# Attention with sixteen-wide heads: the sums over the keys of two key tiles issued one behind the other, with room for four tiles of exponentials

## The chip, the cores and the metric

The kernel runs on one NeuronCore of one Trainium2 chip. The metric is the time of the device for the whole program, in microseconds (us). The kernel before takes 2302.59 us, the median of three runs (2300.83 to 2303.88). All of the program's work is one launch: twelve layers of a decoder, one behind the other.

## The reference, cut to what matters

Twelve sublayers, each `x = x + f(layernorm(x))`, with B = 2 sequences, T = 512 queries and C = 256 channels. Three of them are attentions that this change reaches, all with 16 heads of 16 channels:

```python
# first self attention: causal, with linear position biases (ALiBi)
# third self attention: a band, |i - j| <= 32
band = jnp.abs(idx[:, None] - idx[None, :]) <= WINDOW // 2
scores = jnp.where(band[None, None], scores, -jnp.inf)
attn = jax.nn.softmax(scores, axis=-1)
out = jnp.einsum('bhqk,bhkd->bhqd', attn, v)
...
# last cross attention: 512 queries against 1024 keys, no mask
scores = jnp.einsum('brqd,brkd->brqk', qh, kh) * scale
weights = jax.nn.softmax(scores, axis=-1)
out = jnp.einsum('brqk,brkd->brqd', weights, vh)
```

## The kernel before, in words

The program is a chain of stages with a barrier between them. Within a stage each engine has its own instruction list, written out by hand, and waits on semaphores. Four of the stages are made by `quad_attention_stage` (L3085): `a0a` (first self attention, causal), `a2a` (third self attention, banded), `a2x` (third cross attention, with a full mask, which brings its own buffer `probs`) and `a3x` (last cross attention). The change does nothing in `a2x`.

A stage works through U = 8 units; a unit is one group of four heads of one sequence. A unit has KT key tiles of 128 keys: 4 in `a0a` and `a2a`, 8 in `a3x`. Key tiles are counted through the whole stage as n, up to N = 32, 32 and 64. In a unit three things happen:

- **Rows.** For every query tile and head one matmul gives scores with queries on partitions (`row`, L3233, in the self attentions followed by a mask matmul, L3236), and VectorE takes the maximum of each (`row_maximum`, L3392). These only serve to find the shift of the softmax. They run more than one unit ahead: `lead` rows (44 in `a3x`) are done before the loop. Their results lie in `ring`, three banks of PSUM, so that a row matmul waits until the maximum three places back has been taken (`wait_for_bank`). When a unit's rows are done, VectorE makes `most` (L3398), TensorE turns it (`turn_most`, L3243) and ScalarE negates it (`negate`, L3349) and a DMA puts it into the queries' stack. `turn_most` and a turn of the finished sums (`turn_u`, L3287, read by VectorE at L3413 and L3416) take a place of the ring too.
- **Scores.** For key tile n, in two halves of two heads each, `score(n, half)` (L3260, in the self attentions with the mask at L3265) puts keys on partitions into `scores_T`, which has one place for each half. So the scores of n + 1 wait until ScalarE has taken the exponentials of the same half of n (`exp`, L3336).
- **Sums.** `value(n)` (L3279) multiplies the exponentials with the values, four matmuls (float32, one for each head) that write 32 partitions of `u` each, side by side. After a unit's last tile ScalarE copies `u` out (`u_out`, L3356) before the next unit's first sum may begin.

Everything around the change is set by the order of TensorE's list. For each n and half it is: the scores of n + 1, two rows, `turn_u` or `turn_most` if this is their slot (slot s is 2 times the key tile in the unit plus the half; `turn_u_at` is 4; `turn_most_at` is 10 in `a3x` and 1 in the self attentions), and in the first half the sums of n - 1. The exponentials have R = 3 places in `pT`, so `exp(n, 0)` waits for the sums of n - 3. In `a3x` two float32 weight matrices are also quantised by VectorE behind its last maximum (L3440 to L3456), for which TensorE does one small matmul (L3317) in the third tile from the end.

Of the kernel before, what the change touches and what calls it, by code (L numbers as in the profile page):

```python
# [243 lines left out]

def project_stage(core, name, turned_jobs, value_jobs, values="h d", loads=(), first=(), room=None, R=5,
                  padding=None, rounding=None, early=(), spread=False):
# [21 lines left out]
    with stage(core, name) as st:  # L268
# [9 lines left out]
        if room is None:  # L278
            x32 = st.sb("x32", [P, R, 512])
            left = st.sb("left", [P, R, 512])  # L280
            hml = st.sb("hml", [P, R, 3, 512], BF16)
            vout = st.sb("vout", [P, RV, V]) if value_jobs else None
        else:
            x32, left = (room[:, x * R * 512:(x + 1) * R * 512].rearrange("p (r t) -> p r t", r=R) for x in range(2))
            hml = room[:, R * 1024:R * 1792].bitcast(BF16).rearrange("p (r c t) -> p r c t", r=R, c=3)
            vout = room[:, R * 1792:R * 1792 + RV * V].rearrange("p (r c) -> p r c", r=RV)
# [2798 lines left out]
def quad_attention_stage(core, name, nkey, bufs, q_parts, k_parts, v_scr, ao, keys_of, queries_of, lead, turn_u_at,  # L3085
# [13 lines left out]

    assert len(loads) <= GROUPS * B
    nc = core.nc
    KT = nkey // P
# [3 lines left out]
    N = U * KT  # L3108
    HALVES = 2 * KT
    rows = []  # L3110
    for qt in range(QT):
        k0, n = keys_of(qt)
# [3 lines left out]
    NR = len(rows)  # L3116
    assert NR == 2 * HALVES
    assert nkey // 512 == 1 + max(r[4] for r in rows)
    R = 3
    NSTACK = 16 * (2 * len(RUNS) + (2 if extra else 0))  # L3120
    PER = NR + 2

# [13 lines left out]
    with stage(core, name) as st:  # L3136
# [34 lines left out]
        def first_rows(u, s):  # L3171

            r = lead + NR * u + 2 * s
            return range(r, min(r + 2, U * NR))

        with nc.Block() as block:
# [39 lines left out]
            def _(pe):  # L3216
# [7 lines left out]
                def row(r):  # L3224
                    u, i = divmod(r, NR)
                    qt, h, k0, n, part = rows[i]
                    out = ring[:, row_place(r) % 3, 0:n]
                    if i == 0:
                        stack_ready(pe, u)
                    wait_for_bank(row_place(r))  # L3230
                    lhsT = qs[0:K - 1, u % nbuf, h, qt * P:(qt + 1) * P]
                    rhs = ks[0:K - 1, u % nbuf, h, k0:k0 + n]
                    mm = nc.tensor.matmul(out, lhsT, rhs, start=True, stop=True, skip_group_check=True)  # L3233
                    if key_mask is not None or full is not None:
                        m0, mask = (k0, full[0][:, qt, k0:k0 + n]) if key_mask is None else key_mask(qt)
                        mm = nc.tensor.matmul(out[:, m0 - k0:m0 - k0 + mask.shape[1]], core.ident_bf[:, :], mask,  # L3236
                                              start=False, stop=True, skip_group_check=True)
                    mm.then_inc(rowed, 1)

                def turn_most(u):  # L3240
                    pe.wait_ge(most, u + 1)
                    wait_for_bank(most_place(u))
                    nc.tensor.transpose(ring[0:HG4 * QT, most_place(u) % 3, 0:P], mcol[:, u % 2, :], core.ident[:, :]  # L3243
                                        ).then_inc(most_turned, 1)

                def score(n, half):
                    u, kt = divmod(n, KT)
                    q0, w = queries_of(kt)
                    if kt == 0 and half == 0:
                        stack_ready(pe, u)  # L3250
                        pe.wait_ge(shift_in[u % nbuf], 16 * (u // nbuf + 1))
                    if n and full is not None:
                        pe.wait_ge(masked, 2 * (n - 1) + half + 1)
                        pe.wait_ge(copied, 2 * (n - 1) + half + 1)
                    elif n:
                        pe.wait_ge(expd, 2 * (n - 1) + half + 1)
                    for j in range(2):
                        h = 2 * half + j
                        out = sT[:, half, j, :]
                        mm = nc.tensor.matmul(out[:, 0:w], ks[0:K, u % nbuf, h, kt * P:(kt + 1) * P],  # L3260
                                              qs[0:K, u % nbuf, h, q0:q0 + w], start=True, stop=True,
                                              skip_group_check=True)
                        if query_mask is not None:
                            for m0, mask in query_mask(kt):
                                mm = nc.tensor.matmul(out[:, m0 - q0:m0 - q0 + mask.shape[1]], core.ident_bf[:, :],  # L3265
                                                      mask, start=False, stop=True, skip_group_check=True)
                    mm.then_inc(scored, 1)

                def value(n):
                    u, kt = divmod(n, KT)  # L3270
                    q0, w = queries_of(kt)
                    if kt == 0:
                        pe.wait_ge(v_in[u % 2], 16 * (u // 2 + 1))
                        if u:
                            pe.wait_ge(u_moved, u)
                    pe.wait_ge(expd, 2 * (n + 1))
                    for h in range(HG4):
                        hs = slice(32 * h, 32 * h + 32)
                        mm = nc.tensor.matmul(up[hs, q0:q0 + w], vs[:, u % 2, kt, hs], pT[:, n % R, h, 0:w],  # L3279
                                              start=(kt == 0), stop=True, skip_group_check=True)  # L3280
                    mm.then_inc(valued, 1)
# [17 lines left out]
                for n in range(N):  # L3299
                    u, kt = divmod(n, KT)  # L3300
                    for half in range(2):
                        s = 2 * kt + half
                        if n + 1 < N:
                            score(n + 1, half)
                        for r in first_rows(u, s):
                            row(r)
                        if s == turn_u_at and u:
                            turn_u(u - 1)
                        if s == turn_most_at and u + 1 < U:
                            turn_most(u + 1)  # L3310
                        if half == 0 and n >= 1:
                            value(n - 1)
                        if quant is not None and n == N - 3 and half == 1:
                            pe.wait_ge(weight_step, 2)
                            pe.wait_ge(row_most, U * NR)
                            pe.wait_ge(shift_ready, U)
                            nc.tensor.matmul(sums, core.ones[:, :], part[:, :], start=True, stop=True  # L3317
                                             ).then_inc(weighed, 1)
                value(N - 1)
                turn_u(U - 1)  # L3320

# [594 lines left out]
```

## Time and profile before

| what | us |
|---|---|
| median of three runs | 2302.59 (2300.83 to 2303.88) |
| the profiled execution | 2292.74 |
| its span in the profile | 2290.9 |
| TensorE busy | 1857.9 (81%) |
| VectorE busy | 1476.2 (64%) |
| ScalarE busy | 1072.9 (47%) |
| GpSimd busy | 830.4 (36%) |
| stage `a0a`, from about 45 to 157 | 112 |
| stage `a2a`, from about 1256 to 1344 | 88 |
| stage `a3x`, from about 1949 to 2183 | 234 |

The page gives busy time of each engine over the whole span, which averages over stages with different limits. What bounds the three stages is read from the timeline of each engine: start of each instruction, its length, and in brackets how long its engine sat idle before it and what released it. Matmuls overlap in the pipeline, so the distance of two starts says more than a length.

### The profile page before, as it was taken

Reading aid. Unit: us, or ns where it says so; the run is one execution under the profiler, and the core shown is the slowest. Engines: PE = TensorE matmul, PEld = TensorE weight load, DVE = VectorE, ACT = ScalarE, POOL = GpSimd, SP = SyncE. Lnnn points to the kernel's source line nnn. Section 1 sums busy time; section 2 is a strip of 40 time slices with the busy share of each in tenths; the row PEclk is TensorE's granted clock in tenths of the full one; section 3 lists DMA queues with packets and bytes.
Section 4 is the critical chain, followed back from the end, with each engine's and each line's share of the span. In section 5 each row is a group of like instructions: output and inputs, shape, how many; then the busy total and the mean of one; then the engine's idle time right before and its main releaser. Section 6 shows DMA issues by size and latency. Waiting matters only on the chain. (4 is left out here: it accounts for less than half of the span.)

```text
span 2290.9 us, 32146 instructions
## 1 busy us (share of the span) xinstructions
PE 1857.9 (81%) x11356; PEld 937.0 (41%) x11379; DVE 1476.2 (64%) x2551; ACT 1072.9 (47%) x1818; POOL 830.4 (36%) x751
## 2 busy tenths in 40 slices
PE   5888979999785677677896787999789776999954
PEld 3444423333453444445583552333257433222223
DVE  4643266663766999985435548999454464777676
ACT  2453124444333444542344343888833433366646
POOL 1000035554245999993204012666640412000012
PEclk9999989999986989987898888999889887699977
DMA  6602551210039014003425813332044401443000
GB/s 193 162 26 87 192 174 47 65 46 1 19 103 201 15 30 78 2 1 113 156 73 186 185 54 89 80 70 49 19 176 156 142 10 34 98 95 68 10 1 19
DMA packets 172353, 190.50 MB, mean 83 GB/s; under 512 B 14820, under 2 KB 138799, under 8 KB 171287
## 3 DMA queue, kind: packets, MB, share of 16 engines
q1 hardware_dynamic: 169124, 180.07, 28.5%
q0 software_dynamic: 3072, 8.39, 1.2%
q8 instruction: 93, 1.52, 0.3%
q14 instruction: 64, 0.52, 0.1%
HBM read 124.04 MB, written 68.30 MB: 84 GB/s over the span
## 5 line engine op out<-in xcount | busy, mean ns | idle before, releaser
L3381 POOL TENSOR_TENSOR a2x_masked<-a2x_masked,tall_rows 128x512 f32<-128x512 f32 x128 | 163.3, 1276 | 111.4 <-ACT a2x_masked L3343 111.4
L1398 ACT ACTIVATE experts<-a1x_scores 128x1024 f32<-128x1024 f32 x128 | 124.1, 1021 | 164.5 <-PE a1x_scores L1329 164.5
L3392 DVE TENSOR_REDUCE a3x_row_most<-a3x_ring 128x1 f32<-128x512 f32 x256 | 159.3, 682 | 43.5 <-PE a3x_ring L3233 43.5
L3392 DVE TENSOR_REDUCE a2x_row_most<-a2x_ring 128x1 f32<-128x512 f32 x256 | 162.4, 679 | 7.0 <-DMA pad_scr<-wide_rows 5.3
L1435 POOL TENSOR_TENSOR a1x_tree<-experts 128x1024 f32<-128x1024 f32 x64 | 150.4, 2350 | 32.2 <-ACT experts L1398 32.2
L671 POOL TENSOR_TENSOR a0x_pair_sums<-a0x_probs_T 128x1024 f32<-128x1024 f32 x48 | 114.7, 2390 | 130.1 <-ACT a0x_probs_T L800 102.7
L854 DVE TENSOR_REDUCE ctx_then_heads<-a0x_rows 128x2 f32<-128x1024 f32 x88 | 107.7, 1224 | 82.6 <-PE a0x_rows L689 82.4
L1367 DVE TENSOR_TENSOR experts<-experts,a1x_inverse_total 128x2048 f32<-128x2048 f32 x64 | 145.7, 2276 | 4.2 <-ACT a1x_inverse_total L1411 4.2
L3336 ACT ACTIVATE a3x_probs_T<-a3x_scores_T 128x1024 f32<-128x1024 f32 x128 | 123.2, 1018 | 48.4 <-PE a3x_scores_T L3260 48.4
L1318 PE MATMUL a1x_scores<-a1x_qs,a1x_ks 96*128 96x128 bf16 x1024 | 92.4, 243 | 58.7 <-ACT experts L1398 45.1
L3336 ACT ACTIVATE wide_rows<-a2x_masked 128x1024 f32<-128x1024 f32 x128 | 135.8, 1061 | 1.4 <-POOL a2x_masked L3381 1.4
L800 ACT ACTIVATE a0x_probs_T<-a0x_scores_T 128x1024 f32<-128x1024 f32 x96 | 98.4, 1025 | 77.5 <-PE a0x_scores_T L715 60.5
L1377 DVE TENSOR_REDUCE a1x_most<-a1x_scores 128x128 bf16<-128x2048 f32 x43 | 98.5, 2292 | 33.2 <-PE a1x_scores L1318 33.2
L1329 PE MATMUL a1x_scores<-a1x_most,a1x_minus_ident 128*128 128x512 bf16 x256 | 72.7, 410 | 56.6 <-DVE a1x_most L1383 30.0
L1318 PEld LDWEIGHTS a1x_scores<-a1x_qs,a1x_ks 96*128 96x128 bf16 x1024 | 68.3, 109 | 107.7 <-ACT experts L1398 78.5
L3233 PE MATMUL a2x_ring<-a2x_ks,a2x_qs 97*128 97x512 bf16 x256 | 99.3, 388 | 13.2 <-DMA a2x_qs<-in_ones_bf 10.2
L711 PE MATMUL a0x_scores_T<-ctx_then_heads 64*128 64x512 f32 x384 | 102.3, 611 | 0.7 <-ACT ctx_then_heads L806 0.7
L3404 DVE TENSOR_TENSOR a2x_masked<-a2x_scores_T,tall_rows 128x512 f32<-128x512 f32 x128 | 87.6, 685 | 23.3 <-ACT wide_rows L3336 14.8
L3233 PE MATMUL a3x_ring<-a3x_ks,a3x_qs 96*128 96x512 bf16 x256 | 94.1, 427 | 8.0 <-DMA a3x_qs<-q_scr 8.0
L728 PE MATMUL a0x_u<-a0x_probs_T,a0x_vs 128*64 128x512 f32 x384 | 92.8, 605 | 0.0
L3343 ACT COPY a2x_masked<-a2x_scores_T 128x512 f32<-128x512 f32 x128 | 74.8, 585 | 37.3 <-PE a2x_scores_T L3260 31.1
L1344 PE MATMUL a1x_u<-experts,a1x_vs 128*32 128x128 f32 x2048 | 85.4, 318 | 6.1 <-DVE experts L1367 6.1
(676 smaller groups left out, 4268.3 us busy)
## 6 DMA issues: line engine op xcount, KB each, us to landing
v_scr<-p0x_vout SPq DMA_DIRECT2D x24, 256.0 KB, 2.0
k_scr<-p0x_x SPq DMA_DIRECT2D x24, 256.0 KB, 2.3
ctx_then_heads<-k_scr SPq DMA_DIRECT2D x8, 768.0 KB
a0x_vs<-v_scr SPq DMA_DIRECT2D x8, 768.0 KB, 5.1
experts<-in_L_ffn_w SPq DMA_DIRECT2D x8, 768.0 KB, 6.6
v_scr<-experts SPq DMA_DIRECT2D x16, 256.0 KB, 2.2
a1x_vs<-v_scr SPq DMA_DIRECT2D x16, 256.0 KB, 5.2
v_scr<-m1f_vout SPq DMA_DIRECT2D x16, 256.0 KB, 2.8
```

What stands on the lines that cost most here:

```text
L671: nc.gpsimd.tensor_tensor(pair[:, n // 2 % RP, :, :], pT[:, (n - 1) % R, :, :], pT[:, n % R, :, :], ALU.add).then_inc(paired, 1)
L711: nc.tensor.matmul(sT[:, n % 2, h, :], ks[hs, u % 3, kt * P:(kt + 1) * P], qs[hs, u % 3, :], start=True, stop=False, skip_group_check=True)
L854: nc.vector.tensor_reduce(rm[:, qt, :, c], row_psum(r)[:, :, :], AX.X, ALU.max).then_inc(row_most, 1)
L1318: mm = nc.tensor.matmul(sp_[:, g % 3, i, j, :], ks[0:96, h, kt * P:(kt + 1) * P], qs[0:96, h, qt * P:(qt + 1) * P], start=(j == 0), stop=F ...
L1367: nc.vector.tensor_tensor(ex[:, n % E, :, :], ex[:, n % E, :, :], rp[:, 0, :].unsqueeze(1).to_broadcast([P, H, P]), ALU.mult).then_inc(nor ...
L1377: nc.vector.tensor_reduce(mx[:, n % 2, :], src, AX.X, ALU.max).then_inc(most, 1)
L1398: nc.scalar.activation(ex[:, n % E, 8 * half:8 * half + 8, :], sp_[:, g % 3, :, :, :].rearrange("p i j q -> p (i j) q"), ACT.Exp).then_inc ...
L1435: nc.gpsimd.tensor_tensor(tree[:, :, :], e[:, 0:8], e[:, 8:16], ALU.add).then_inc(folded, 1)
L3233: mm = nc.tensor.matmul(out, lhsT, rhs, start=True, stop=True, skip_group_check=True)
L3336: nc.scalar.activation(pT[:, n % R, 2 * half:2 * half + 2, 0:w], src, ACT.Exp).then_inc(expd, 1)
L3381: nc.gpsimd.tensor_tensor(sm[:, i % 2, 1, :], sm[:, i % 2, 1, :], full[1][:, i // 2 % KT, :], ALU.add).then_inc(pool_masked, 1)
L3392: nc.vector.tensor_reduce(rm[:, u % 2, h * QT + qt:h * QT + qt + 1, part], ring[:, row_place(r) % 3, 0:n], AX.X, ALU.max).then_inc(row_mos ...
```

## The change

Where the stage has its own buffer of exponentials (`a0a`, `a2a`, `a3x`), the buffer has four places in place of three, and TensorE issues the sums of two key tiles together: in the first half of every even n the sums of n - 2 and n - 1, and none at odd n. At the end the sums of the last two tiles follow. Lines move by one to six.

```diff
-    R = 3
+    R = 4 if probs is None else 3
...
-                        if half == 0 and n >= 1:
+                        if half == 0 and probs is not None and n >= 1:
+                            value(n - 1)
+                        if half == 0 and probs is None and n >= 2 and n % 2 == 0:
+                            value(n - 2)
                             value(n - 1)
...
+                if probs is None:
+                    value(N - 2)
                 value(N - 1)
                 turn_u(U - 1)
```

TensorE's list in `a3x` about the turn of the maxima, before (L3260 scores, L3233 rows, L3279 sums, L3243 `turn_most`):

```order
L3279 MATMUL a3x_u<-a3x_probs_T,a3x_vs 32x512 x4
L3260 MATMUL a3x_scores_T<-a3x_qs,a3x_ks 128x512 x2
L3233 MATMUL a3x_ring<-a3x_ks,a3x_qs 128x512 x2
L3260 MATMUL a3x_scores_T<-a3x_qs,a3x_ks 128x512 x2
L3233 MATMUL a3x_ring<-a3x_ks,a3x_qs 128x512 x2
L3243 MATMUL a3x_ring<-ident,a3x_most 16x128
L3279 MATMUL a3x_u<-a3x_probs_T,a3x_vs 32x512 x4
L3260 MATMUL a3x_scores_T<-a3x_qs,a3x_ks 128x512 x2
```

The same place in the changed kernel, on to the next sums (L3261, L3234, L3280, L3244 are the same lines, moved by one):

```order
L3280 MATMUL a3x_u<-a3x_probs_T,a3x_vs 32x512 x8
L3261 MATMUL a3x_scores_T<-a3x_qs,a3x_ks 128x512 x2
L3234 MATMUL a3x_ring<-a3x_ks,a3x_qs 128x512 x2
L3261 MATMUL a3x_scores_T<-a3x_qs,a3x_ks 128x512 x2
L3234 MATMUL a3x_ring<-a3x_ks,a3x_qs 128x512 x2
L3244 MATMUL a3x_ring<-ident,a3x_most 16x128
L3261 MATMUL a3x_scores_T<-a3x_qs,a3x_ks 128x512 x2
L3234 MATMUL a3x_ring<-a3x_ks,a3x_qs 128x512 x2
L3261 MATMUL a3x_scores_T<-a3x_qs,a3x_ks 128x512 x2
L3234 MATMUL a3x_ring<-a3x_ks,a3x_qs 128x512 x2
L3280 MATMUL a3x_u<-a3x_probs_T,a3x_vs 32x512 x8
```

Before, four rows lay between one tile's sums and the next, and one tile's sums stood directly behind `turn_most`. Now eight rows lie between two pairs of sums, and behind `turn_most` come scores.

The end of `a3x`, where no rows are left, TensorE before:

```order
L3279 MATMUL a3x_u<-a3x_probs_T,a3x_vs 32x512 x4
L3260 MATMUL a3x_scores_T<-a3x_qs,a3x_ks 128x512 x4
L3279 MATMUL a3x_u<-a3x_probs_T,a3x_vs 32x512 x4
L3260 MATMUL a3x_scores_T<-a3x_qs,a3x_ks 128x512 x4
L3279 MATMUL a3x_u<-a3x_probs_T,a3x_vs 32x512 x4
```

and in the changed kernel:

```order
L3280 MATMUL a3x_u<-a3x_probs_T,a3x_vs 32x512 x8
L3261 MATMUL a3x_scores_T<-a3x_qs,a3x_ks 128x512 x8
L3280 MATMUL a3x_u<-a3x_probs_T,a3x_vs 32x512 x8
L3261 MATMUL a3x_scores_T<-a3x_qs,a3x_ks 128x512 x8
```

Two halves of scores between the sums have become four. The lists of the other engines keep their order.

## Rows read from the trace of the kernel before

**Rows 1.** The page, busy time of each engine over the span.
```profile
PE 1857.9 (81%) x11356; PEld 937.0 (41%) x11379; DVE 1476.2 (64%) x2551; ACT 1072.9 (47%) x1818; POOL 830.4 (36%) x751
```

**Rows 2.** Windows of `a0a`, `a2a`, `a3x`: length, busy of PE, PEld, DVE, ACT, POOL, clock, DMA.
```profile
45.00:157.00 112.00, 92.83 (x808) 47.28 (x808) 61.05 (x152) 50.20 (x82) 0.00 (x0) 0.92 0.49 121
1256.00:1344.00 88.00, 73.15 (x808) 49.13 (x808) 44.20 (x150) 35.52 (x82) 0.00 (x0) 0.87 0.64 158
1949.00:2183.00 234.00, 215.07 (x1068) 58.98 (x1069) 176.84 (x290) 129.51 (x147) 0.00 (x0) 0.92 0.29 65
```

**Rows 3.** Timeline of PE in `a3x`, one regular key tile: start, length, instructions.
```profile
2069.11 1.06 PE L3279 MATMUL a3x_u<-a3x_probs_T,a3x_vs 128*32 128x512 f32 x8
2070.11 0.60 PE L3260 MATMUL a3x_scores_T<-a3x_qs,a3x_ks 97*128 97x512 bf16 x2
2070.55 0.60 PE L3233 MATMUL a3x_ring<-a3x_ks,a3x_qs 96*128 96x512 bf16 x2
2070.98 0.59 PE L3260 MATMUL a3x_scores_T<-a3x_qs,a3x_ks 97*128 97x512 bf16 x2
...
2072.03 1.07 PE L3279 MATMUL a3x_u<-a3x_probs_T,a3x_vs 128*32 128x512 f32 x8
```

**Rows 4.** The same timeline in cuts: second pass of the sums; the fourth row.
```profile
2069.56 0.61 PE L3279 MATMUL a3x_u<-a3x_probs_T,a3x_vs 128*32 128x512 f32 x4
...
2071.72 0.39 PE L3233 MATMUL a3x_ring<-a3x_ks,a3x_qs 96*128 96x512 bf16 x1
```

**Rows 5.** Timeline of DVE in the same stretch.
```profile
2070.97 2.48 DVE L3392 TENSOR_REDUCE a3x_row_most<-a3x_ring 128x1 f32<-128x512 f32 x4 [0.44 <-PE a3x_ring L3233]
2073.89 0.69 DVE L3392 TENSOR_REDUCE a3x_row_most<-a3x_ring 128x1 f32<-128x512 f32 x1 [0.45 <-PE a3x_ring L3233]
```

**Rows 6.** Timelines of PE and ACT in `a3x` about the turn of the maxima.
```profile
2075.46 0.28 PE L3243 MATMUL a3x_ring<-ident,a3x_most 128*16 128x128 f32 x1 [0.43 <-DVE a3x_most L3398]
2075.67 1.06 PE L3279 MATMUL a3x_u<-a3x_probs_T,a3x_vs 128*32 128x512 f32 x8
2077.00 0.61 PE L3260 MATMUL a3x_scores_T<-a3x_qs,a3x_ks 97*128 97x512 bf16 x2 [0.27 <-ACT a3x_probs_T L3336]
...
2078.93 1.06 PE L3279 MATMUL a3x_u<-a3x_probs_T,a3x_vs 128*32 128x512 f32 x8
...
2075.95 1.00 ACT L3336 ACTIVATE a3x_probs_T<-a3x_scores_T 128x1024 f32<-128x1024 f32 x1
```

**Rows 7.** Timeline of PE in `a3x` where one unit's sums end.
```profile
2058.66 1.07 PE L3279 MATMUL a3x_u<-a3x_probs_T,a3x_vs 128*32 128x512 f32 x8
...
2061.36 0.61 PE L3260 MATMUL a3x_scores_T<-a3x_qs,a3x_ks 97*128 97x512 bf16 x2 [0.66 <-ACT a3x_probs_T L3336]
```

**Rows 8.** Timelines of PE and ACT in the last unit of `a3x`, without rows.
```profile
2157.78 1.04 PE L3260 MATMUL a3x_scores_T<-a3x_qs,a3x_ks 97*128 97x512 bf16 x4
...
2161.95 0.39 PE L3260 MATMUL a3x_scores_T<-a3x_qs,a3x_ks 97*128 97x512 bf16 x1
...
2158.43 2.99 ACT L3336 ACTIVATE a3x_probs_T<-a3x_scores_T 128x1024 f32<-128x1024 f32 x3 [0.42 <-PE a3x_scores_T L3260]
```

**Rows 9.** Timelines of PE and DVE at the end of `a3x`.
```profile
2174.17 0.28 PE L3317 MATMUL a3x_ring<-a3x_weight_part,ones 128*128 128x2 f32 x2
...
2179.43 0.65 PE L3287 MATMUL a3x_ring<-ident,a3x_u_sb 128*128 128x128 f32 x4 [0.71 <-ACT a3x_u_sb L3356]
...
2181.83 0.25 DVE L3413 RECIPROCAL a3x_inverse<-a3x_ring 128x16 f32<-128x16 f32 x1
```

**Rows 10.** Timeline of PE in `a0a`, start of a unit.
```profile
115.74 0.28 PE L3243 MATMUL a0a_ring<-ident,a0a_most 128*16 128x128 f32 x1 [0.36 <-DVE a0a_most L3398]
117.06 0.28 PE L3260 MATMUL a0a_scores_T<-a0a_qs,a0a_ks 103*128 103x256 bf16 x1 [1.05 <-ACT a0a_probs_T L3336]
```

**Rows 11.** Timeline of PE in `a2a`, the one long wait.
```profile
1317.10 0.29 PE L3260 MATMUL a2a_scores_T<-a2a_qs,a2a_ks 97*128 97x160 bf16 x1 [2.95 <-issue]
```

## The prediction

> **What bounds the kernel now.** I read the page first: TensorE is busy 81% of the span, VectorE 64% [rows 1]. That is an average; the change touches three stages, so the windows of those come next [rows 2]. In each TensorE is the busiest engine: 92.8 of 112 us in `a0a`, 73.2 of 88 in `a2a`, 215.1 of 234 in `a3x`. But in `a3x` VectorE has 176.8 us of its own, and the two are coupled through a ring of three banks. So the timeline of a regular key tile in `a3x` decides. Its period is 2.93 us, from the sums at 2069.11 to those at 2072.03 [rows 3], and it can be walked through as one loop over two engines:
>
> - sums start to the next scores: 1.00 (2069.11 to 2070.11) [rows 3];
> - scores to the first maximum on VectorE: 0.86 (2070.11 to 2070.97) [rows 3, 5];
> - that maximum to the fourth row, which waits for its bank: 0.75 (2070.97 to 2071.72) [rows 4, 5];
> - fourth row to the sums: 0.32 (2071.72 to 2072.03) [rows 3, 4].
>
> Together 2.93. VectorE's four maxima take (2.48 - 0.68) / 3 = 0.60 from start to start, 0.68 being one alone [rows 5], so it works 2.48 of the 2.93 and idles 0.44 while the sums run. The slack of VectorE is thin, and the reader should see that it lies exactly in the time of the sums.
>
> **What the change gives: one change of array shape less per pair.** Matmuls of 512 columns start 0.22 apart (two scores from 2070.11, two rows from 2070.55, two scores from 2070.98) [rows 3]. From the fourth row to the sums it is 0.32, so 0.10 is lost on entering. The sums are two passes, the second 0.45 after the first (2069.11, 2069.56) [rows 3, 4]. The next scores come 0.55 after the start of the second pass, so about 0.10 is lost on leaving. A second tile's sums directly behind the first should start like a further pass: 0.45 + 0.45 = 0.91, where alone it would cost 0.91 + 0.10 + 0.10. So a pair saves 0.20, if nothing else is in the way. No row shows one tile's sums behind another's at full pace; the bounds are 0.91 (pass behind pass) and 1.10 (as when alone). I take 0.91, since the two passes already load different weights.
>
> The fourth place for exponentials costs no instruction. It removes a possible wait of ScalarE for the sums three tiles back, which now come up to a tile later; I put it at nothing either way. VectorE, GpSimd and the queues keep their lists; the DMAs of SP wait for scores or sums of a whole unit and move along with these.
>
> **`a3x`, regular pairs: slower by 0.38.** Eight rows now lie between two pairs of sums. The ring holds three, so the eighth row must wait for the fifth maximum. Walking the same loop: sums to scores 0.91 + 1.00, scores to first maximum 0.86, to the end of the fifth 0.75 + 4 x 0.60 = 3.14, to the sums 0.32. That is 6.23, against 2 x 2.93 = 5.85. TensorE alone would be there sooner: sixteen matmuls of 0.22 and the entering give 3.6 from the scores where the loop gives 0.86 + 3.14 + 0.32 = 4.32. What happened is plain: during two tiles of sums VectorE has at most three banks of work, 1.8 us, and it gets nothing new for 1.91 + 0.86. Its idle time per two tiles rises from 0.88 to 1.35, and TensorE waits for it later.
>
> **`a3x`, the pair with `turn_most`: slower by 0.91.** There the chain first maximum, `most`, turn, negate, exponential, scores takes 3.11 (2073.89 to 2077.00) [rows 5, 6]. Before, a tile's sums (2075.67) lay inside it, while ScalarE worked at 2075.95, and TensorE still idled 0.27. Now scores stand there, waiting for the same exponential, and the sums are paid elsewhere at 0.91. The rest is the same length in both: 1.00 + 0.86 ahead, 1.92 from 2077.00 to the sums at 2078.93.
>
> **`a3x`, the pair at the end of a unit: about +0.06.** Sums to the scores behind `u_out` take 2.70 (2058.66 to 2061.36) [rows 7]. Now: 0.91 + 2.70 + 0.86 + 0.75 + 2 x 0.60 for the eighth row, 0.60 for the bank of `turn_u`, 0.56 for it and the entering: 7.58. Before: from 2058.66 to 2.93 ahead of 2069.11, which is 7.52.
>
> A unit of eight tiles has two regular pairs and one of each other: 0.76 + 0.91 + 0.06 = 1.73. Rows last for 53 of the 64 tiles, 6.5 units: **+11.2 us**.
>
> **`a3x`, the last five pairs, without rows: 0.89 each.** Before, two tiles take 4.17 (2157.78 to 2161.95) [rows 8]; ScalarE needs 4 x 0.92 = 3.7 of it, and one tile's sums always run beside its exponentials. Now: a pair of sums 1.91, the scores behind it and their landing 0.65, an exponential 0.92, a second to its end 1.05, the last scores and entering 0.53: 5.06. **+4.4 us.** Against this the end of the stage: VectorE's quantising starts with the small matmul at 2174.17 and holds up the last reciprocal until 2181.83, 7.66 later, though TensorE's turn was done at 2179.43 + 0.65 = 2180.08 [rows 9]. Now the small matmul stands one place further from the end, 6.9 ahead of the turn's end (by 1.0, since one tile's sums moved behind it), so 1.0 of those 1.75 is hidden: **-1.0**. `a3x` in all: +14.6.
>
> **`a0a` and `a2a`: faster.** Maxima are shorter here (128 to 512 columns in `a0a`, at most 192 in `a2a`) and each row has two matmuls, so VectorE is busy only half of the window [rows 2] and the ring does not bind on a pair. Seven units keep rows: 14 pairs x 0.20 = -2.7 in each (0.19 before rounding). In `a0a` TensorE also waits 0.36 for VectorE ahead of `turn_most` in each unit, with 1.05 for ScalarE behind it [rows 10]; the sums that stood ahead of this place now follow the 512-column rows, VectorE gets these earlier, and I take this 0.36 as gone in seven units: -2.5. The last units have no rows, and by the same count as in `a3x` three and a half pairs each cost more: 0.5 each in `a0a` (widths of 320 on average, where 512 cost 0.89), 0.3 in `a2a`: +1.8 and +1.1. So **`a0a` -3.4, `a2a` -1.5**. In `a2a` TensorE waits 2.95 once for a DMA [rows 11]; if that landing does not come earlier with the rest, half of the gain is lost: 0.8.
>
> **The sum.** +14.6 - 3.4 - 1.5 = +9.7. Against the profiled execution's 2292.74 that is 2302.4; the median of the runs stands 9.85 above that execution, and I expect the same of the changed kernel: **2312.3 us**, slower by 0.42%.
>
> The Trainium skill warns of this side: TensorEngine Tiling (Array Packing), Performance Considerations, PSUM Bottleneck, says that tiling speeds up TensorE and not the emptying of PSUM, which may then bound. By it the pairs in `a3x` gain nothing or lose, and those in the self attentions keep their gain; the trace agrees, with 0.60 a maximum in `a3x` and VectorE half idle in `a0a` and `a2a` [rows 2, 5]. The page has a rule for the other side too, which stands with the first rival.
>
> **Rivals.**
>
> *Faster, the ring does not bind.* If VectorE kept its pace through the pair, all 64 pairs would save 0.20, and nothing would be lost at the turns: -12.6, so 2290. For it: TensorE is the busiest engine everywhere, 0.20 per pair is in the trace. Against it: the eighth row's wait. It decides at a maximum of (5.85 - 3.09 - 0.15) / 5 = 0.52 per start, 3.09 being 1.91 + 0.86 + 0.32 and 0.15 a maximum's tail and wait; above it a pair loses, and 0.60 is measured. The Trainium skill has the rule for this rival: TensorEngine Tiling (Array Packing), Key Properties, says that a change of tiling mode drains TensorE. The 0.10 on entering and on leaving agree. Chance 0.04.
>
> *Slower still, the second sums cost as much as alone.* Then 1.10 in place of 0.91, 64 times: +12.3 more, 2325. Half of it, 2318, is as likely. For it: no row of such a sequence. Against it: pass behind pass at 0.45. Chance 0.10 together.
>
> *Hardly slower.* Part of the loss in `a3x` is not there: if TensorE's wait for the turn's chain is filled, or VectorE's lateness in `a0a` gives back more, `a3x` falls to about +8 and the sum to +3: 2306. Chance 0.08, and 0.03 of it below 2304.
>
> *The change does not do what it says.* The order of both programs excludes it: eight sums in one row where four stood.
>
> **How the numbers follow.** Forecast 2308 to 2317 with 0.78; the rivals 0.04, 0.10 and 0.08. The range that leaves two in ten out is 2306 to 2320: it takes in half of the rival on the second sums, and the bounds of `a0a` and `a2a` (nothing gained there gives 2317). A measurement of this kernel tells about 0.2%, 4.6 us, from no change: faster than 2298.0 has 0.04, between 2298.0 and 2307.2 has 0.08, slower 0.88.
>
> **What would show each step.** In `a3x`: sums of 16 records whose third pass starts 0.45 after the second; a regular pair of 6.2; the eighth row released by VectorE; idle of TensorE of about 1 us behind `turn_most`, ended by ScalarE; two tiles in 5.06 at the end; a window of some 248 us. In `a0a` some 108.5 and no wait ahead of `turn_most`. The prediction is wrong if a regular pair in `a3x` is below 5.85, or if the sums of a pair take 2.1.

## The result

The changed kernel takes 2314.53 us (median of seven runs, against 2303.88 for seven runs of the kernel before beside it); the ratio is 1.0057 with a 95% interval of 1.0032 to 1.0083, so +13.1 us, between +7.4 and +19.1. The prediction said +9.7 and 2312.3. One of the seven executions took 9211 us and is left out of the ratio. The profiled execution is a long one, 2328.88, so its length is no measure and only single stretches are read from it. A second profiled execution of the same kernel (the first experiment) took 2313.5 in its span.

The page of the changed kernel, engines over the span, answers to [rows 1]:

```profile
PE 1872.6 (80%) x11356; PEld 948.5 (41%) x11379; DVE 1474.7 (63%) x2551; ACT 1071.6 (46%) x1818; POOL 831.0 (36%) x751
```

The same instructions, and the same work on VectorE and ScalarE. Windows about `a0a`, `a2a` and `a3x` in it answer to [rows 2]; columns as there:

```profile
44.00:156.00 112.00, 90.43 (x808) 48.32 (x808) 61.74 (x152) 49.93 (x82) 0.00 (x0) 0.92 0.52 121
1260.00:1348.00 88.00, 70.20 (x812) 50.88 (x812) 44.58 (x152) 36.38 (x83) 0.40 (x2) 0.88 0.62 161
1955.00:2220.00 265.00, 232.57 (x1070) 65.34 (x1070) 175.56 (x290) 129.43 (x147) 0.10 (x1) 0.85 0.24 57
```

All of the loss is in `a3x`. From its first matmul to its last it was 230.1 us before; here it is 262.0, and 248.7 in the second execution.

**A regular pair.** Timeline of PE in `a3x` of the changed kernel, from one pair of sums to the next; beside [rows 3]:

```profile
2054.04 1.92 PE L3280 MATMUL a3x_u<-a3x_probs_T,a3x_vs 128*32 128x512 f32 x16
2055.90 0.61 PE L3261 MATMUL a3x_scores_T<-a3x_qs,a3x_ks 97*128 97x512 bf16 x2
2056.34 0.60 PE L3234 MATMUL a3x_ring<-a3x_ks,a3x_qs 96*128 96x512 bf16 x2
2056.78 0.59 PE L3261 MATMUL a3x_scores_T<-a3x_qs,a3x_ks 97*128 97x512 bf16 x2
2057.21 0.69 PE L3234 MATMUL a3x_ring<-a3x_ks,a3x_qs 96*128 96x512 bf16 x2
2057.74 0.60 PE L3261 MATMUL a3x_scores_T<-a3x_qs,a3x_ks 97*128 97x512 bf16 x2
2058.17 0.38 PE L3234 MATMUL a3x_ring<-a3x_ks,a3x_qs 96*128 96x512 bf16 x1
2058.70 0.39 PE L3234 MATMUL a3x_ring<-a3x_ks,a3x_qs 96*128 96x512 bf16 x1 [0.15 <-DVE a3x_row_most L3398]
2058.93 0.60 PE L3261 MATMUL a3x_scores_T<-a3x_qs,a3x_ks 97*128 97x512 bf16 x2
2059.36 0.38 PE L3234 MATMUL a3x_ring<-a3x_ks,a3x_qs 96*128 96x512 bf16 x1
2059.90 0.39 PE L3234 MATMUL a3x_ring<-a3x_ks,a3x_qs 96*128 96x512 bf16 x1 [0.15 <-DVE a3x_row_most L3398]
2060.22 0.64 PE L3280 MATMUL a3x_u<-a3x_probs_T,a3x_vs 128*32 128x512 f32 x4
```

The period is 6.18, against 5.85 for two single tiles. The sixth and the eighth row stand alone in their rows because they wait for VectorE. The same timeline cut at the third and at the fourth pass of the sums, and VectorE (DVE) in the stretch:

```profile
2054.93 0.61 PE L3280 MATMUL a3x_u<-a3x_probs_T,a3x_vs 128*32 128x512 f32 x4
...
2055.35 0.61 PE L3280 MATMUL a3x_u<-a3x_probs_T,a3x_vs 128*32 128x512 f32 x4
...
2056.76 4.28 DVE L3398 TENSOR_REDUCE a3x_row_most<-a3x_ring 128x1 f32<-128x512 f32 x7 [1.60 <-PE a3x_ring L3234]
```

The third pass starts 0.89 and the fourth 1.31 after the first, at 2054.04. So the passes behind the first step of 0.45 follow at 0.43, also from one tile to the other, and the second tile's sums cost 0.86 and not 0.91 (1.86 from the pair's start to the scores at 2055.90, where one tile's took 1.00). VectorE starts at 2056.76, 0.86 behind the scores, and then works without a break; from its start to the eighth row it is 3.14, as the prediction has it.

**The turn of the maxima.** PE and ACT, beside [rows 6]:

```profile
2064.50 0.28 PE L3244 MATMUL a3x_ring<-ident,a3x_most 128*16 128x128 f32 x1 [0.43 <-DVE a3x_most L3404]
2066.04 1.03 PE L3261 MATMUL a3x_scores_T<-a3x_qs,a3x_ks 97*128 97x512 bf16 x2 [1.26 <-ACT a3x_probs_T L3342]
...
2064.99 1.90 ACT L3342 ACTIVATE a3x_probs_T<-a3x_scores_T 128x1024 f32<-128x1024 f32 x2
```

TensorE idles 1.26 where it did a tile's sums before. And something else is there: two scores take 1.03 and not 0.61. The windows on either side show why; the clock is the number behind POOL:

```profile
2059.00:2065.90 6.90, 5.20 (x30) 1.42 (x28) 5.30 (x10) 2.51 (x5) 0.00 (x0) 1.00 0.02 4
2065.90:2072.70 6.80, 6.66 (x24) 1.63 (x24) 2.58 (x4) 3.04 (x4) 0.00 (x0) 0.50 0.00 1
```

The granted clock is 0.50, 1.2 GHz, for 6.8 us, from the end of the idle on. Such falls came in five units in a row of this execution, and a sixth came where the rows end:

```profile
2185.40:2192.20 6.80, 6.05 (x22) 1.14 (x23) 0.00 (x0) 3.53 (x4) 0.00 (x0) 0.50 0.00 1
```

Four of the five units take 30.8 or 30.9, where one without a fall takes 27.7 and one of the kernel before 26.1 (distances of a unit's first exponential to the next unit's).

### The profile page after: what moved, and what is told of

Same layout as the page of the kernel before. It is cut to its first block and busy times, and to the rows that moved or that the text cites. A ratio compares the mean times of both kernels' runs of the same rounds, so it can differ in the third digit from the quotient of the medians.

```text
span 2327.0 us, 32143 instructions
## 1 busy us (share of the span) xinstructions
PE 1872.6 (80%) x11356; PEld 948.5 (41%) x11379; DVE 1474.7 (63%) x2551; ACT 1071.6 (46%) x1818; POOL 831.0 (36%) x751
## 5 line engine op out<-in xcount | busy, mean ns | idle before, releaser
L1318 PEld LDWEIGHTS a1x_scores<-a1x_qs,a1x_ks 96*128 96x128 bf16 x1024 | 70.3, 111 | 107.2 <-ACT experts L1398 77.9
L3234 PE MATMUL a3x_ring<-a3x_ks,a3x_qs 96*128 96x512 bf16 x256 | 102.6, 448 | 12.9 <-DMA a3x_qs<-q_scr 8.0
L3234 PE MATMUL a2x_ring<-a2x_ks,a2x_qs 97*128 97x512 bf16 x256 | 99.1, 387 | 13.3 <-DMA a2x_qs<-in_ones_bf 10.3
L3261 PE MATMUL a3x_scores_T<-a3x_qs,a3x_ks 97*128 97x512 bf16 x256 | 84.3, 417 | 17.7 <-ACT a3x_probs_T L3342 17.7
```

Of the source, the lines that this page charges most:

```text
L1318: mm = nc.tensor.matmul(sp_[:, g % 3, i, j, :], ks[0:96, h, kt * P:(kt + 1) * P], qs[0:96, h, qt * P:(qt + 1) * P], start=(j == 0), stop=F ...
```

## Experiments

Stage lengths below run from the first matmul of a stage to its last. The theory has three parts, all in `a3x`: the ring of three banks starves VectorE during a pair; the sums leave the shadow of the turn's chain; and in the last unit ScalarE starves. Against these it sets 0.20 saved per pair. The rivals are named in each expectation.

**The changed kernel once more.** No edit.

> The changed kernel once more. Its first profiled execution has three events at which the granted clock of TensorE falls to half for 6.8 us that repeat in every unit of a3x, and a window of 262 us for the stage where the step by step count gave 248.6. If these falls always come with the idle behind turn_most, this execution has a3x at 260 us or more again and the program at about 2328. If they come in some executions only, this one has a3x near 248 and the program near 2313, with regular pairs of 6.2 us and 1.5 us of idle behind turn_most as before.

Measured: ratio 1.0065 (1.0038 to 1.0093), median 2313.4. `a3x` 248.7, regular pairs 6.17, idle behind `turn_most` 1.26. The long falls of the clock come in some executions only; in this one there are three falls, of 3.4 us each. Two of them in windows:

```profile
2062.60:2066.00 3.40, 3.40 (x19) 0.70 (x17) 1.84 (x4) 1.15 (x2) 0.00 (x0) 0.50 0.00 0
2175.20:2178.60 3.40, 3.40 (x17) 0.57 (x10) 0.00 (x0) 0.95 (x2) 0.00 (x0) 0.51 0.00 0
```

The idles of 1.26 ended at 2061.09 and 2173.49, 1.5 and 1.7 ahead of these. The other four turns have the same idle of 1.26 and no fall behind it. A unit with a short fall took 29.3, so such a fall costs 1.6. This execution also has the last unit clean; PE from one pair of sums to the next there, beside [rows 8]:

```profile
2187.97 1.92 PE L3280 MATMUL a3x_u<-a3x_probs_T,a3x_vs 128*32 128x512 f32 x16
2189.83 1.04 PE L3261 MATMUL a3x_scores_T<-a3x_qs,a3x_ks 97*128 97x512 bf16 x4
2191.55 0.60 PE L3261 MATMUL a3x_scores_T<-a3x_qs,a3x_ks 97*128 97x512 bf16 x2 [0.68 <-ACT a3x_probs_T L3342]
2192.46 0.61 PE L3261 MATMUL a3x_scores_T<-a3x_qs,a3x_ks 97*128 97x512 bf16 x2 [0.31 <-ACT a3x_probs_T L3342]
2193.00 1.92 PE L3280 MATMUL a3x_u<-a3x_probs_T,a3x_vs 128*32 128x512 f32 x16
```

5.03 for two tiles, 4.17 before: the exponentials follow the scores one by one while no sums are left to fill TensorE.

**Pairs in the self attentions alone.**

```diff
-    R = 4 if probs is None else 3
+    paired = probs is None and KT == 4
+    R = 4 if paired else 3
...
-                        if half == 0 and probs is not None and n >= 1:
+                        if half == 0 and not paired and n >= 1:
...
-                        if half == 0 and probs is None and n >= 2 and n % 2 == 0:
+                        if half == 0 and paired and n >= 2 and n % 2 == 0:
...
-                if probs is None:
+                if paired:
                     value(N - 2)
```

> Pairs and four places in a0a and a2a alone; a3x as in the kernel before. Theory (array shape changes saved, VectorE not in the way in these two stages): a0a shorter by 3.4 and a2a by 1.5, so 4.9 us below the kernel before. Rival (the self attentions wait for ScalarE and the DMA queue and give nothing back): within 1 us of the kernel before, and the whole of the change's loss is then smaller in a3x than counted.

Measured: ratio 0.9985 (0.9969 to 1.0002), -3.4 us, between -7.1 and +0.5. That holds both the theory's -4.9 and nothing. The profile is clearer. A regular unit of `a0a` takes 11.3 where it took 12.1, the wait of 0.36 ahead of `turn_most` [rows 10] is gone in the turns of the third to seventh unit, and a unit of `a2a` takes 8.4 for 8.8. But one wait in `a0a`, of scores that need what DMAs bring (queries, keys and shift of the unit), is longer than in the profile before:

```profile
88.05 0.59 PE L3262 MATMUL a0a_scores_T<-a0a_qs,a0a_ks 103*128 103x512 bf16 x1 [4.03 <-issue]
```

The next run, which has no pairs in `a0a`, has it too:

```profile
87.77 0.59 PE L3262 MATMUL a0a_scores_T<-a0a_qs,a0a_ks 103*128 103x512 bf16 x1 [4.16 <-issue]
```

So it does not need the pairs. It stands in all thirteen profiled executions, 0.44 to 6.06 long (1.25 in the kernel before), and it always ends 40.7 to 43.1 us behind the stage's first matmul. Ahead of it the sixteen DMA engines are busy all the time; a window of the kernel before, with their share (1.11) and GB/s last:

```profile
73.00:85.00 12.00, 10.36 (x100) 5.34 (x97) 7.56 (x20) 6.13 (x10) 0.00 (x0) 1.00 1.11 275
```

So what TensorE saves ahead of this wait, in the first units, it waits away again, and mostly the units behind it can shorten the stage. `a2a` has such a wait too, of 1.65 to 5.13, which ends 58.3 to 61.4 behind its first matmul in all thirteen. With a wait of some 4 in both, `a0a` takes 111.7 here and 114.6 in the next run: 2.9 less, for 3.4 forecast. `a2a` takes 88.4 here, 87.9 and 86.6 in the kernel before and the next run, which have no pairs there, and 85.5 and 86.7 in the two of the changed kernel: its DMA waits vary by more than the pairs give.

**Pairs in `a3x` alone.** As above with `KT == 8`.

> Pairs and four places in a3x alone. Theory (ring of three banks, turn's chain, last unit): a3x longer by 14.6 without falls of the clock, so about 2318, and by up to 32 with them. Rival (the pairs are neutral in a3x, and what was lost is lost in the self attentions): within 2 us of the kernel before.

Measured: ratio 1.0078 (1.0051 to 1.0104), +17.9, between +11.7 and +23.9; `a3x` 248.7, as in the kernel with all pairs. The loss is all here. The number is larger than the change's +13.1, but the intervals overlap widely, and with the -3.4 of the run before it makes +14.5.

**The turn behind a pair of sums.**

```diff
-                                 queries_of=lambda kt: (0, T), lead=44, turn_u_at=4, turn_most_at=10, **stack,
+                                 queries_of=lambda kt: (0, T), lead=44, turn_u_at=4, turn_most_at=12, **stack,
```

> The changed kernel with turn_most of a3x in slot 12 in place of 10, so that a pair of sums stands directly behind it again. Theory (the chain of turn, negate and exponential costs 0.91 per unit only because no sums lie in its shadow): 7 us below the changed kernel, about 2307, TensorE's idle behind turn_most gone, and with it any fall of the clock at this place. Rival (ring alone): the idle only moves to another place, within 2 us of the changed kernel.

Measured: ratio 1.0007 (0.9992 to 1.0023), 2302.63: 10.8 below the changed kernel's 2313.4, and `a3x` 238.5, 10.2 less. PE about the turn:

```profile
2054.90 0.27 PE L3244 MATMUL a3x_ring<-ident,a3x_most 128*16 128x128 f32 x1 [0.30 <-DVE a3x_row_most L3398]
2055.10 1.92 PE L3280 MATMUL a3x_u<-a3x_probs_T,a3x_vs 128*32 128x512 f32 x16
2056.95 0.61 PE L3261 MATMUL a3x_scores_T<-a3x_qs,a3x_ks 97*128 97x512 bf16 x2
```

The scores behind the pair no longer wait. The pair that holds the turn takes 6.96, for 7.75 in the changed kernel and 6.89 before. Two of the three falls of the clock are gone with the idle; one is left in the last unit. A unit takes 26.9 for 27.7: 0.8, where the theory has 0.91. The remainder of the 10.2 is the falls and the end of the stage. The regular pairs stay at 6.17: the rival (ring alone) was right about these and wrong about the rest, since the idle did not come back elsewhere. That the falls went with the idle rests on one profiled execution of this kernel.

**Three places for exponentials.**

```diff
-    R = 4 if probs is None else 3
+    R = 3
```

> The changed kernel with three places for exponentials in place of four. Theory: the fourth place hides nothing; ScalarE's exponentials of a tile would wait for the first of the two sums, but at that time ScalarE has the second half of the tile before to do, so a3x, a0a and a2a keep their lengths within 1 us each (a3x 248.7 from first to last matmul, as in the second look at the changed kernel). Rival: ScalarE is held in each pair, the scores behind the pair come late, and a3x grows by 0.3 per pair or more, 10 us.

One execution: 2319.97, `a3x` 248.7 and every unit of it as in the changed kernel to 0.1, `a0a` 111.6, `a2a` 86.5. The fourth place hides nothing here. The total is from one execution and says no more.

**Maxima at half their size, sums single and in pairs.** Both runs have `turn_most_at=12` in `a3x`, and there take each maximum over 256 of the 512 columns, which leaves that part of the maxima out. The first is the kernel before with these edits, the second the changed kernel.

```diff
                     nc.vector.tensor_reduce(rm[:, u % 2, h * QT + qt:h * QT + qt + 1, part],
-                                            ring[:, row_place(r) % 3, 0:n], AX.X, ALU.max).then_inc(row_most, 1)
+                                            ring[:, row_place(r) % 3, 0:(n // 2 if quant is not None else n)], AX.X, ALU.max).then_inc(row_most, 1)
```

> Sums one tile at a time, as before, but turn_most of a3x in slot 12, and VectorE takes each maximum in a3x over 256 of the 512 columns (the shift of the softmax is then the maximum over half of the keys; this leaves work out). A maximum then takes 0.33 from start to start in place of 0.60. TensorE is the bound of a regular key tile: two tiles in 5.66, and a3x about 26 less rows' time at the start, some 207 to 212 us. It is the partner of the next run.

> The changed kernel's order with turn_most of a3x in slot 12 and maxima in a3x over 256 of 512 columns (leaves the same work out). Theory (0.20 saved per pair where the ring does not bind, by the count it stops binding below 0.52 per maximum): regular pairs of 5.48 against 5.66 in the run before, a3x shorter than there by about 5, the last unit still longer by 3.5. Rival (the loss of a pair has nothing to do with VectorE's pace): regular pairs here are again 0.3 to 0.4 longer than two single tiles.

Measured: 2274.31 single (ratio 0.9878, 0.9852 to 0.9905), 2264.74 in pairs (0.9843, 0.9819 to 0.9867). `a3x` 206.3 and 201.2. PE and DVE of the first in a regular tile:

```profile
2042.95 1.06 PE L3279 MATMUL a3x_u<-a3x_probs_T,a3x_vs 128*32 128x512 f32 x8
...
2045.79 0.64 PE L3279 MATMUL a3x_u<-a3x_probs_T,a3x_vs 128*32 128x512 f32 x4
...
2044.81 0.76 DVE L3392 TENSOR_REDUCE a3x_row_most<-a3x_ring 128x1 f32<-128x256 f32 x2 [1.21 <-PE a3x_ring L3233]
```

and of the second in a regular pair:

```profile
2020.30 1.92 PE L3280 MATMUL a3x_u<-a3x_probs_T,a3x_vs 128*32 128x512 f32 x16
...
2025.24 0.60 PE L3234 MATMUL a3x_ring<-a3x_ks,a3x_qs 96*128 96x512 bf16 x2
2025.76 0.64 PE L3280 MATMUL a3x_u<-a3x_probs_T,a3x_vs 128*32 128x512 f32 x4
...
2023.02 3.39 DVE L3398 TENSOR_REDUCE a3x_row_most<-a3x_ring 128x1 f32<-128x256 f32 x8 [1.89 <-PE a3x_ring L3234]
```

Single tiles follow each other at 2.83 or 2.84, so two take 5.67; a pair takes 5.46. With VectorE out of the way the same pair that lost 0.32 gains 0.21, and its rows wait for nobody. This settles the ring: the sign of a pair turns with the length of a maximum. The place of the turn, slot 12 in both of these runs, is not what does it: with slot 12 and whole maxima (the run with the turn behind a pair) a regular pair takes 6.17. One 128x256 maximum takes 0.34 from start to start (0.42 alone, two in 0.76), as both expectations had it with 0.33. The last unit still loses as before (24.0 against 20.9 in its last stretch).

**Rows ahead of scores.** A slot's two rows in front of its scores in the three stages. Three kernels: pairs for the first 24 of 32 tiles in the self attentions and single sums in `a3x`; the changed kernel's pairs everywhere; single sums everywhere.

```diff
-                        if n + 1 < N:
+                        if n + 1 < N and full is not None:
                             score(n + 1, half)
                         for r in first_rows(u, s):
                             row(r)
+                        if n + 1 < N and full is None:
+                            score(n + 1, half)
```

> A version meant to beat both: pairs in a0a and a2a up to the last unit, single sums in a3x, and in these three stages the two rows of a slot ahead of the slot's scores, so that VectorE gets work 0.43 earlier after the sums. By the step by step count: the period of a regular key tile in a3x falls from 2.93 to TensorE's own 2.83 and less is idle at the turns, about -10 in a3x, -9 in a0a, -5 in a2a; DMA waits in the self attentions may take a third of their part. About 2280. Rival: ScalarE's exponentials come 0.43 later and TensorE waits for them instead; then within 3 us of the kernel before.

> The changed kernel with the two rows of a slot ahead of its scores in a0a, a2a and a3x. Theory (a pair loses because VectorE gets nothing for the sums and the scores behind them): VectorE's first maximum comes 0.42 after the pair in place of 0.86, so a3x falls by about 11.6 from 248.7 (first to last matmul) to 237, still 19 above the single order with rows first (217.9). Rival (the order of rows and scores does not matter for a pair): a3x stays at 248.

> The kernel before with rows ahead of scores in the three stages, sums one tile at a time everywhere. a3x as in the version meant to beat both, 217.9 from first to last matmul. In a0a and a2a single sums cost 2.8 and 2.4 more than pairs up to the last unit by the step by step count. So about 2280, 5 us above that version. Rival (the pairs give nothing in the self attentions once rows stand first): the two are equal within 1 us.

| kernel | median us | ratio to the kernel before | `a0a` | `a2a` | `a3x` |
|---|---|---|---|---|---|
| some pairs, rows first | 2274.67 | 0.9884 (0.9863 to 0.9906) | 105.5 | 84.3 | 217.9 |
| all pairs, rows first | 2289.22 | 0.9956 (0.9942 to 0.997) | 106.3 | 85.8 | 232.8 |
| no pairs, rows first | 2272.88 | 0.988 (0.9864 to 0.9897) | 107.2 | 81.8 | 217.9 |

The first and the third beat both kernels, by some 27 us the kernel before. They cannot be told apart, though the pairs save 0.4 in a unit of `a0a` (10.7 for 11.1) and of `a2a` (7.9 for 8.3): what they save ahead of the DMA landings is waited away, and the DMA waits of `a2a` vary by more than that. So the rival of the third expectation stands for the total.

Of the first expectation, `a3x` gave 12.2 for 10, `a0a` 5.7 for 9 and `a2a` 3.6 for 5. Where it comes from was not where I put it. PE of the first kernel in a regular tile of `a3x`:

```profile
2044.98 1.06 PE L3281 MATMUL a3x_u<-a3x_probs_T,a3x_vs 128*32 128x512 f32 x8
2045.98 0.60 PE L3235 MATMUL a3x_ring<-a3x_ks,a3x_qs 96*128 96x512 bf16 x2
2046.42 0.60 PE L3262 MATMUL a3x_scores_T<-a3x_qs,a3x_ks 97*128 97x512 bf16 x2
2046.85 0.69 PE L3235 MATMUL a3x_ring<-a3x_ks,a3x_qs 96*128 96x512 bf16 x2
2047.38 0.60 PE L3262 MATMUL a3x_scores_T<-a3x_qs,a3x_ks 97*128 97x512 bf16 x2
2047.90 1.07 PE L3281 MATMUL a3x_u<-a3x_probs_T,a3x_vs 128*32 128x512 f32 x8
```

Still 2.92, not 2.83: the fourth row now waits for its bank just as long, with scores between it and the sums. The gain is at the turns: the two tiles about `turn_most` take 6.12 for 6.89, those about a unit's end 6.65 for 7.52, so a unit 24.5 for 26.1. With all pairs it is the same. PE from one pair of sums to the next, and DVE between them:

```profile
2025.80 0.60 PE L3234 MATMUL a3x_ring<-a3x_ks,a3x_qs 96*128 96x512 bf16 x2
...
2030.12 1.48 PE L3280 MATMUL a3x_u<-a3x_probs_T,a3x_vs 128*32 128x512 f32 x9
...
2026.22 4.88 DVE L3400 TENSOR_REDUCE a3x_row_most<-a3x_ring 128x1 f32<-128x512 f32 x8 [1.17 <-PE a3x_ring L3234]
```

VectorE starts 0.42 behind the pair's end, as the second expectation had it, and yet the regular pair stays at 6.18 (2023.94 to 2030.12): what the loop wins there it gives back between the eighth row and the sums, where two scores now stand. The gain is at the turns alone (25.8 a unit for 27.7). `a3x` came out at 232.8, 15.9 lower for 11.6 expected, so that expectation had the sign for the stage and the wrong place.

The three stages together are 21.5 and 22.3 shorter than in the profiled execution of the kernel before, in the first and the third kernel. Where the rest of the 27 comes from is not shown.

**Single sums in the last units.** Scores first, `a3x` as before, pairs in the self attentions for tiles 0 to 23 and single sums in the last two units. Against the kernel before:

```diff
-    R = 3
+    R = 4 if KT == 4 else 3
+    last_pair = N - 8 if KT == 4 else 0
...
-                        if half == 0 and n >= 1:
+                        if half == 0 and n > last_pair:
+                            value(n - 1)
+                        if half == 0 and 2 <= n <= last_pair and n % 2 == 0:
+                            value(n - 2)
                             value(n - 1)
```

> Scores first as in the kernel before, a3x as before, pairs in a0a and a2a up to tile 24 and single sums in the last unit. Theory (pairs cost in the last unit, where no rows are left and ScalarE needs a tile's sums beside its exponentials): last unit of a0a back from 10.2 to 9.5 (its last stretch) and of a2a from 8.3 to 7.9, together some 1.8 below pairs throughout the self attentions, 5 to 7 below the kernel before. Rival: no difference from pairs throughout.

Measured: ratio 0.9968 (0.9955 to 0.9981), -7.4, between -10.4 and -4.4. The last stretches are 9.5 and 7.9 as expected, `a0a` 108.8, `a2a` 85.2. This is the one version in which the change's own idea, alone, is faster by more than its interval. Against pairs throughout the self attentions (-3.4) it is 4 better, of which the last stretches show 1.1 (9.5 for 10.2 and 7.9 for 8.3); the intervals of the two overlap, and the rest is not shown.

## Why the prediction was right, point by point

- **The sign and the place.** The sign was clear of the interval. The loss in `a3x` is shown by the run with pairs there alone (+17.9). The gain in `a0a` is shown by its units (11.3 for 12.1); in time the run without pairs in `a3x` has -3.4 with an interval that holds nothing, and the version with single sums in the last units has -7.4.
- **Regular pairs, +0.38.** Measured 6.17 or 6.18 for 6.23, so +0.32. The loop over the two engines was right in each step; only the second sums cost 0.86 and not 0.91, since passes follow at 0.43 behind the first step of 0.45. That also puts the bound of 1.10, and the rival built on it, out.
- **0.20 saved where the ring does not bind.** Measured 0.21 (5.67 to 5.46) with short maxima. The bound of 0.52 per maximum lies between the 0.34 that gains and the 0.60 that loses.
- **The turn, +0.91.** Measured 7.75 for 6.89, +0.86; undone by moving the turn.
- **The end of a unit, +0.06.** Measured 7.60 for 7.52.
- **A unit, +1.73.** Measured 27.7 for 26.1, +1.6.
- **The last unit, +0.89 a pair.** Measured 5.03 for 4.17, +0.86. The last reciprocal came at 2204.68, 7.66 after the small matmul, as before; it stood 0.65 behind the turn's end (2203.38 + 0.65) for 1.75 before. The -1.0 was -1.1. PE and DVE at the end of the second execution, beside [rows 9]:

```profile
2197.02 0.28 PE L3321 MATMUL a3x_ring<-a3x_weight_part,ones 128*128 128x2 f32 x2
...
2203.38 0.65 PE L3288 MATMUL a3x_ring<-ident,a3x_u_sb 128*128 128x128 f32 x4 [0.71 <-ACT a3x_u_sb L3362]
...
2204.68 0.25 DVE L3419 RECIPROCAL a3x_inverse<-a3x_ring 128x16 f32<-128x16 f32 x1
```

- **`a3x` in all, +14.6.** This term was too small: +18.6 to the last matmul, less 1.1 for the hidden end, is +17.5 in the usual execution, and +30.8 in the first profiled one. What was missing is a term: the granted clock. The sum took all work at 2.4 GHz behind the start of the stage, as it was before. Three short falls at 1.6 are 4.8. Without them `a3x` would be +12.7, so the other terms were 1.9 too large together, each a little (the points above). The six long falls make the 262.0: 18.1 above 248.7 less 4.8.
- **`a0a` -3.4, `a2a` -1.5.** The parts per unit came out (-0.8 of -0.74 in `a0a`, -0.4 in `a2a`; the 0.36 gone, as taken), the totals less. In the two executions of the changed kernel `a0a` takes 111.0 and 111.4, for 111.2 before and not 108.5. Two things were wrong in the sum. It let seven units gain, while what is saved ahead of the wait that ends at 41 to 43 us is waited away; the forecast allowed for such a loss in `a2a` alone. And it counted 17.5 pairs of 16: with `lead` at 30 in these stages, 98 of the 128 rows remain, which last for 24.5 of 32 tiles, so 12 pairs have rows and not 14, beside the three and a half without. That is 0.4 too much gain in each stage (and -2.7 + 1.1 is -1.6, not -1.5). Forecast -4.9, measured -3.4 with an interval that holds both.
- **What was luck.** The mechanism in `a3x` was right place by place, but the total is near for a poorer reason: falls of the clock, put at nothing, cost 4.8 in the usual execution, and the other terms of `a3x` were 1.9 too large; the self attentions gave back 1.5 less than forecast. Two of the thirteen executions of the changed kernel were long ones (2328.88, with the six long falls, and 2330.11, not profiled), outside the range of 2306 to 2320.

## What to carry to other kernels

Before work on the busiest engine is bunched to save its switches, count what the bunch withholds from the engine that it feeds: here 0.20 saved per pair became 0.32 lost, because VectorE, with at most three banks of work, ran dry during 1.86 us of sums, and TensorE waited for it later at the ring. How much work the fed engine has decides: with maxima of 0.34 in place of 0.60 the same pair gained 0.21. A long piece of work next to a chain of waits is worth its whole length there, so a reordering has to be checked at every place where the old order hid something, not only in the regular period; and the order of small things behind the long one (rows ahead of scores) was worth some 27 us in all, more than the whole change cost. And what TensorE saves ahead of a DMA landing that does not move is not saved.

## What had not been expected of the hardware

- TensorE's granted clock fell to half, 1.2 GHz, within `a3x` with pairs. With the turn at its place behind an odd tile and scores first, TensorE idles 1.26 behind each of seven turns, with 0.42 to 0.95 ahead of it; a fall came at six of the seven in the first execution and at three in the second (at the same three with pairs in `a3x` alone and with three places), beginning within the idle of 1.26 or at most 1.8 behind its end. With all pairs and rows first the idle behind the turn is 0.32 in six units and 1.26 in one, and the one fall stands at the 1.26. With the turn ahead of a pair none stands there; the one fall left is behind an idle of 1.10 in the last unit. That idle stands in the executions with single sums too, without a fall. So the falls went and came with the idle at the turn, but what besides it decides is open. The same program had six falls of 6.8 us in one execution and three of 3.4 in the next, so the cost is +18 or +4.8 from execution to execution. The Trainium skill, TensorE: Matmul & The Clock Gate, HAM oscillation, tells of a kernel whose clock falls at every one of its DMA waits between bursts of matmuls. By the same section of the Trainium skill those waits are of 3 to 5 us. These runs agree in that falls stand at waits; they differ in that the waits here are of 0.43 and 1.26 us, and that most of the turns in the usual execution have them without a fall.
- The same happened in `a0a` with single sums in one execution (the first run with half maxima): seven falls of 3.4, and five units at 13.6 or more, where the kernel before shows 12.1 in most of them with the same order on TensorE. Idle there is 0.37 and 1.05 about its turn. None of the executions with pairs in `a0a` repeats it from unit to unit. That the pairs protect `a0a` is possible; it was not tried.
- Float32 sums over 32 columns each, four side by side, follow at 0.43 per pass of 512 columns (0.45 behind the first pass of a group), whether the next pass belongs to the same tile or to another; going in costs 0.10 and coming out 0.12 (the scores at 2055.90 stand 0.55 behind the last pass, at 2055.35). Here the number type changes together with the array's shape, but a place in the changed kernel tells them apart, where scores (bfloat16, whole array), the turn of the sums (float32, whole array) and sums (float32, 32 columns) follow each other. PE in the second execution, then cut at the last matmul of the turn:

```profile
2187.00 0.60 PE L3261 MATMUL a3x_scores_T<-a3x_qs,a3x_ks 97*128 97x512 bf16 x2 [0.31 <-ACT a3x_probs_T L3342]
2187.44 0.60 PE L3288 MATMUL a3x_ring<-ident,a3x_u_sb 128*128 128x128 f32 x4
...
2187.77 0.27 PE L3288 MATMUL a3x_ring<-ident,a3x_u_sb 128*128 128x128 f32 x1
```

  The turn starts 0.44 behind the first of two scores, 0.22 a matmul as among scores alone, so the change of type costs nothing there. Its four matmuls start 0.11 apart, but the sums at 2187.97 start 0.20 behind the last of them: 0.09 is lost where only the shape changes.
